# Edge sums in batches of four tiles, and a node ranking moved to another stage

## The reference

```python
# graph convolution of layer 0
agg[dst] = sum over edges (x @ W)[src] / sqrt(deg)
# attention layers (layers 1 and 2 have two each, layer 3 one)
w    = exp(e - m[dst])                       # one factor per edge and head
z    = segment_sum(w, dst)
out  = segment_sum(w[:, :, None] * xW[src], dst) / z[dst]
```

```python
perm = jnp.argsort(deg + deg_noise, stable=True)
```

## Time and profile before

| | |
|---|---|
| time, median of 3 runs | 10034.75 us (10032.0 to 10036.96) |
| span of the profiled execution | 10033.8 us |
| mean granted TensorE clock, share of 2.4 GHz | 0.734 |
| TensorE busy | 7411.3 us, 74% |
| VectorE busy | 5241.3 us, 52% |
| ScalarE busy | 2745.4 us, 27% |
| GpSimd busy | 3592.3 us, 36% |

### The profile page before, as it was taken

How to read it: one execution, slowest core, us unless ns; L and a number is a source line. 1 busy time by engine, 2 the same in 40 slices (tenths; PEclk the granted TensorE clock), 3 DMA queues, 4 the chain that set the end, 5 groups by cost and what they waited for, 6 DMA issues and landing times. The chain is left out here.

```text
span 10033.8 us, 106861 instructions
## 1 busy us (share of the span) xinstructions
PE 7411.3 (74%) x29302; PEld 4772.6 (48%) x29302; DVE 5241.3 (52%) x12836; ACT 2745.4 (27%) x6151; POOL 3592.3 (36%) x3597
## 2 busy tenths in 40 slices
PE   6867686996686596799679849848467469947756
PEld 6833333444454465477456536624223256623334
DVE  7832674225887556301475655555399575543221
ACT  0122000223674232122244314312232144412211
POOL 3715573002573574200536537600100236600111
PEclk5578656998898575799865557568689765568878
DMA  4200332002563432154233233300000133300012
GB/s 109 66 6 13 103 105 63 29 29 78 155 203 113 124 104 59 42 173 159 79 99 92 73 113 110 89 2 15 28 0 0 41 113 93 92 22 4 8 64 80
DMA packets 439924, 740.35 MB, mean 74 GB/s; under 512 B 172477, under 2 KB 268700, under 8 KB 437426
## 3 DMA queue, kind: packets, MB, share of 16 engines
q0 software_dynamic: 182080, 437.26, 15.8%
q1 hardware_dynamic: 239123, 276.05, 8.7%
q10 hardware_dynamic: 18136, 20.19, 0.6%
HBM read 659.96 MB, written 72.93 MB: 73 GB/s over the span
## 5 line engine op out<-in xcount | busy, mean ns | idle before, releaser
L2490 DVE TENSOR_TENSOR acc<-acc,PS 125x256 f32 (+4 forms) x2080 | 883.3, 425 | 1122.4 <-PE PS L2512 1043.3
L2448 POOL DMA_INDIRECT R<-table,edges x1248 | 1210.4, 970 | 611.3 <-issue 317.2
L2511 PEld LDWEIGHTS PS<-TW,hot 128*125 128x125 f32 x3328 | 852.3, 293 | 678.3 <-DVE hot L2470 549.6
L2448 POOL DMA_INDIRECT room<-table,edges x832 | 797.0, 958 | 588.1 <-PE PS L2512 552.3
L2512 PE MATMUL PS<-room,hot 128*125 128x256 f32 x1664 | 995.1, 701 | 0.0
L2512 PE MATMUL PS<-R,hot 128*125 128x256 f32 x1664 | 843.2, 612 | 106.1 <-DVE hot L2470 43.9
L2511 PE MATMUL PS<-TW,hot 128*125 128x1 f32 (+3 forms) x3328 | 762.7, 300 | 46.7 <-DVE hot L2470 15.6
L2464 ACT ACTIVATE R<-R,TW 128x128 f32<-128x128 f32 (+1 forms) x1664 | 611.0, 419 | 414.8 <-DMA R<-table,edges 408.8
L2470 DVE TENSOR_TENSOR hot<-iota,edges 128x125 f32<-128x125 f32 x2496 | 705.9, 284 | 31.3 <-PEq L71 30.5
L2268 PE MATMUL PS<-S,hotT 125*128 125x100 bf16 (+1 forms) x6240 | 352.7, 215 | 450.3 <-DVE hotT L2375 439.7
L2464 ACT ACTIVATE room<-room,TW 128x64 f32<-128x64 f32 x1664 | 479.1, 339 | 657.6 <-DMA room<-table,edges 654.9
(11 more groups left out here) (703 smaller groups left out, 12923.5 us busy)
## 6 DMA issues: line engine op xcount, KB each, us to landing
rowb<-slo_row SPq DMA_DIRECT2D x260, 250.0 KB
W<-in_L_ffn_W1p SPq DMA_DIRECT2D x32, 1024.0 KB
W<-in_L_ffn_W2p SPq DMA_DIRECT2D x32, 1024.0 KB
near<-dst_row SPq DMA_DIRECT2D x98, 256.0 KB
R<-table,edges POOLq DMA_INDIRECT x1248, 2.8
W<-in_L_ffn_w SPq DMA_DIRECT2D x16, 1024.0 KB
room<-table,edges POOLq DMA_INDIRECT x832, 2.8
hib<-hi_mask SPq DMA_DIRECT2D x260, 50.0 KB, 5.9
```

The source lines that it names most:

```text
L2448: pool.indirect_dma_start(self.R[:, u, 0:self.W], None, self.table[:, :], bass.IndirectOffsetOnAxis(ap=self.G.edges[:, g, 0:1], axis=0)).t ...
L2490: v.tensor_tensor(to, to, self.G.PS[0:P, k, 0:self.WH], ALU.add).then_inc(self.put, 1)
L2511: pe.matmul(self.G.PS[0:P, k, self.W:self.WH], self.hot[g % HOT][:, :], self.TW[:, g, :], start=True, stop=True)
```

## The change

- One-hot matrices of four tiles (`TB`) are made by one instruction of 500 elements, two batches ahead, in three buffers.
- VectorE scales its heads of four tiles in one instruction (512 elements in S3 and S5). In S1 it now has two heads of four, 1,024 elements, and ScalarE two. The instruction waits for all four tiles to have landed.
- The factors are copied into `R` behind the rows in all attention passes, by VectorE, and TensorE has one product per tile instead of two in the narrow ones. S1 has three pairs of banks instead of two.
- VectorE's order is now: one-hots of batch `b + 2`, factors and scaling of `b + 1`, the four adds of `b`.
- In the narrow passes and S0 TensorE makes a product of constants (bf16, 500 columns, into PSUM bank 7, which nobody reads) after every tile, and 16 of them at the start.
- The ranking moves from S0 to `bn_ffn`: its key row is stored and loaded after expert 1's weights have been issued, and each of 25 steps is halved (`below`, `above`) and put behind the add of a chunk, from chunk 2 to chunk 51.

```diff
-HOT, TB = 12, 4
+HB, TB = 3, 4
@@ bn_ffn, SyncE and TensorE
                             sp.dma_start(W[j][l][:, :, :], ...).then_inc(loaded[j], 16)
+                        if e == 1:
+                            ranking.sync(sp)
...
+                ranking.tensor(pe)
@@ bn_ffn, VectorE
+                ranking.start(v)
...
                             v.wait_ge(out_done, n + 1)
+                            if 2 <= n < 2 + 2 * T:
+                                (ranking.above if n % 2 else ranking.below)(v, (n - 2) // 2)
                         v.sem_inc(exp_done, 1)
+                ranking.finish(v)
+                v.tensor_copy(G.place[:, :], place[:, :])
@@ EdgeSums
-        self.banks = 2 if self.wide else 5
+        self.banks = 3 if self.wide else 5
-        self.split = 0 if H == 1 else 1 if self.wide else H // 2
+        self.split = 0 if H <= 1 else H // 2
+    def one_hots(self, v, b):
+        if b >= HB:
+            v.wait_ge(self.summed, (b - HB + 1) * TB)
+        v.tensor_tensor(self.hot[b % HB][:, :, :], self.G.iota[:, :].unsqueeze(1).to_broadcast([128, TB, P]),
+                        self.G.edges[:, b * TB:(b + 1) * TB, 2:3].bitcast(F32).to_broadcast([128, TB, P]),
+                        ALU.is_equal).then_inc(self.hot_done, 1)
+    def scale(self, v, b):
+        if not self.H:
+            return
+        g, n = b * TB, self.split
+        u = g % self.slots
+        if g >= self.slots:
+            v.wait_ge(self.summed, g + TB - self.slots)
+        v.tensor_copy(self.R[:, u:u + TB, self.W:self.WH], self.TW[:, g:g + TB, :]).then_inc(self.tails, 1)
+        if n:
+            for j in range(TB):
+                self.landed(v, g + j)
+            r = self.R[:, u:u + TB, 0:n * self.C].rearrange("p t (h c) -> p t h c", h=n)
+            v.tensor_tensor(r, r, self.TW[:, g:g + TB, 0:n].unsqueeze(3).to_broadcast([128, TB, n, self.C]), ALU.mult).then_inc(self.low, 1)
@@ EdgeSums.tensor
-            if self.H:
-                pe.matmul(self.G.PS[0:P, k, self.W:self.WH], self.hot[g % HOT][:, :], self.TW[:, g, :], start=True, stop=True)
-            mm = pe.matmul(self.G.PS[0:P, k, 0:self.W], self.hot[g % HOT][:, :], self.R[:, u, :], start=True, stop=True)
+            mm = pe.matmul(self.G.PS[0:P, k, 0:self.WH], hot, self.R[:, u, :], start=True, stop=True)
         mm.then_inc(self.summed, 1)
+        if not self.wide:
+            keep_clock(pe, self.G)
+def keep_clock(pe, G):
+    pe.matmul(G.PS[:, 7, 0:4 * P], G.ident_b[:, :], G.iota_b[:, :].unsqueeze(1).to_broadcast([128, 4, P]), start=True, stop=True)
@@ aggregate, VectorE and TensorE
-                for g in range(3):
-                    sums.one_hot(v, g)
-                for g in range(ET):
-                    if g + 3 < ET:
-                        sums.one_hot(v, g + 3)
-                    sums.scale(v, g)
-                    if g:
-                        sums.add(v, g - 1)
-                    if ranking and g % 15 == 14 and g >= 30 and (g - 30) // 15 < T:
-                        ranking.step(v, (g - 30) // 15)
+                sums.one_hots(v, 0)
+                sums.one_hots(v, 1)
+                sums.scale(v, 0)
+                for b in range(NB):
+                    if b + 2 < NB:
+                        sums.one_hots(v, b + 2)
+                    if b + 1 < NB:
+                        sums.scale(v, b + 1)
+                    for g in range(b * TB, (b + 1) * TB):
+                        sums.add(v, g)
...
+                for _ in range(0 if sums.wide else 16):
+                    keep_clock(pe, G)
```

More of the change, by code:

```diff
@@ L1069, in bn_ffn @@
         V = lambda x: G.small("L0_ffn_" + x)
+        place = s.sb("place", [P, T])
+        ranking = Ranking(G, s, G.key, place)
         with nc.Block() as block:
@@ L1196, in step, with below @@
     def step(self, v, t):
+        self.below(v, t)
+        self.above(v, t)
+    def below(self, v, t):
         if t == 0:
@@ L1205, in step, with above @@
             c(v.tensor_scalar(junk[:, 0:a], row[:, 0:a], k, 0.0, ALU.is_le, ALU.add, accum_out=part[:, 0, t:t + 1]))
+        c(v.tensor_scalar(junk[:, a:b], row[:, a:b], k, 0.0, ALU.is_lt, ALU.add, accum_out=part[:, 2, t:t + 1]))
+    def above(self, v, t):
+        c, row, junk, part = self.c, self.row, self.junk, self.part
+        k = self.key[:, t:t + 1]
+        a, b = t * P, (t + 1) * P
         if t < T - 1:
             c(v.tensor_scalar(junk[:, b:N], row[:, b:N], k, 0.0, ALU.is_lt, ALU.add, accum_out=part[:, 1, t:t + 1]))
-        c(v.tensor_scalar(junk[:, a:b], row[:, a:b], k, 0.0, ALU.is_lt, ALU.add, accum_out=part[:, 2, t:t + 1]))
         c(v.scalar_tensor_tensor(out=junk[:, a:b], in0=row[:, a:b], scalar=k, in1=self.G.after[0:P, 0:P],
@@ L2430, in __init__ @@
         self.wide = self.WH > 512
-        self.banks = 2 if self.wide else 5
+        self.banks = 3 if self.wide else 5
         self.C = W // H if H else W
-        self.split = 0 if H == 1 else 1 if self.wide else H // 2
-        width = self.WH if self.wide else W
+        self.split = 0 if H <= 1 else H // 2
         if room is None:
-            self.R = s.sb("R", [128, slots, width])
+            self.R = s.sb("R", [128, slots, self.WH])
         else:
-            self.R = room[:, 0:slots * width].rearrange("p (u w) -> p u w", u=slots)
-        self.hot = [s.sb(f"hot{j}", [128, P]) for j in range(HOT)]
+            self.R = room[:, 0:slots * self.WH].rearrange("p (u w) -> p u w", u=slots)
+        self.hot = [s.sb(f"hot{j}", [128, TB, P]) for j in range(HB)]
         self.got = [s.sem(f"got{j}") for j in range(slots)]
@@ L2456, in scalar @@
             return
-        u, W, C = g % self.slots, self.W, self.C
-        if self.wide and g % TB == 0:
-            if g >= self.slots:
-                act.wait_ge(self.summed, g + TB - self.slots)
-            act.activation(self.R[:, u:u + TB, W:self.WH], self.TW[:, g:g + TB, :], ACT.Copy).then_inc(self.tails, 1)
+        u, C = g % self.slots, self.C
         self.landed(act, g)
@@ L2492, in tensor @@
     def tensor(self, pe, g):
-        u, k, half = g % self.slots, g % self.banks, self.WH // 2
-        pe.wait_ge(self.hot_done, g + 1)
+        u, k, half, b = g % self.slots, g % self.banks, self.WH // 2, g // TB
+        hot = self.hot[b % HB][:, g % TB, :]
+        pe.wait_ge(self.hot_done, b + 1)
         if self.H:
-            if self.wide:
-                pe.wait_ge(self.tails, g // TB + 1)
+            pe.wait_ge(self.tails, b + 1)
             pe.wait_ge(self.high, g + 1)
         if self.split:
-            pe.wait_ge(self.low, g + 1)
+            pe.wait_ge(self.low, b + 1)
         if not self.H:
@@ L2506, in tensor, with aggregate @@
             for a in range(2):
[L2507 to L2512 removed]
+                mm = pe.matmul(self.G.PS[0:P, 2 * k + a, 0:half], hot, self.R[:, u, a * half:(a + 1) * half], start=True, stop=True)
+        else:
+            mm = pe.matmul(self.G.PS[0:P, k, 0:self.WH], hot, self.R[:, u, :], start=True, stop=True)
         mm.then_inc(self.summed, 1)
[L2516 removed]
+        if not self.wide:
+            keep_clock(pe, self.G)
+def keep_clock(pe, G):
+    pe.matmul(G.PS[:, 7, 0:4 * P], G.ident_b[:, :], G.iota_b[:, :].unsqueeze(1).to_broadcast([128, 4, P]), start=True, stop=True)
+def aggregate(nc, G, sums, early=0, own=None):
+    NB = ET // TB
     with Stage(nc) as s:
@@ L2721, in _ @@
             def _(v):
-                v.tensor_tensor(key[:, :], G.out_deg[:, :], G.noise[:, :], ALU.add).then_inc(steps, 1)
+                v.tensor_tensor(G.key[:, :], G.out_deg[:, :], G.noise[:, :], ALU.add).then_inc(steps, 1)
                 v.tensor_scalar(dg[:, 0, :], G.out_deg[:, :], 1.0, None, ALU.max).then_inc(steps, 1)
```

29 lines of the change are left out of this document (3 added, 26 removed).

## The result

The changed kernel takes 9929.4 us (median; 9928.09 to 9936.44), the kernel before 10,035.3: ratio 0.9896, 95% interval 0.9882 to 0.991. That is 106 us less, where 46 were forecast.

A forecast was written before the change was run, and what follows sets the result against it. GpSimd's gathers, at least 1.25 us a tile, were taken to set the pace, except in S3 and S5, held by TensorE. Terms: -164 passes, +16 ranking, +102 held gathers = -46, so 9,988 (median 9,989); range 9,885 to 10,085.

The forecast's parts named there:

- their new length: S3 and S5: gathers come down to 1.258 us a tile; -75 and -71 us with 10 each for held gathers.
- the high clock held: TensorE, all six passes: products of constants keep the granted clock near 1.00, so a tile stays under 1.25 us.
- their ends: S3 and S5: last add 16 us after the last gather began, instead of 34.5 and 39.8; -18.5 and -24 us.
- the rule for held gathers: Gathers behind long VectorE operations last longer by operation's end less own start less 0.12 us; +102 over the passes.
- VectorE's batch in S1: S1: a VectorE batch takes 5.2 us, 1.30 a tile, level with 1.29 before; VectorE becomes co-bound.
- The seven borders: Gated network: seven of 50 ranking halves lie on the path at expert borders, where ScalarE waits for `cur`; +16 us.
- rival 1: All passes: long VectorE operations miss the gathers nearly everywhere; -148 + 20, about 9,906 us; chance 0.23.
- S1 42: S1: gathers held by long VectorE operations, hit or miss by chance, add 42 us, VectorE's own 1.30 hiding a part.
- +6: S1 without held gathers: 6 us longer with its end, as VectorE's batch becomes co-bound.
- a mean gather above 1.05 us in S1: Sign for S1: gathers' mean above 1.05 us; a mean of 0.95 would make the forecast wrong.
- The start products: Sixteen products at a pass's start take 6.7 us at the low clock; S2 to S5 start 5.3 us later each, S0 nothing.
- its sum for a tile at the low clock: TensorE, narrow passes: 1.27 - 0.33 + 0.42 + about 0.1 = 1.46 us a tile, over 1.25, so the clock decides.

The follow-up runs named there:

- padded run: The changed kernel with eight more copies of 128x16 per batch on VectorE in S1, into tiles nobody reads: 9998.6 us, S1 613.8 us.
- the split alone: The changed kernel with one head of S1 on VectorE and three on ScalarE, instead of two and two: 9939.5 us, S1 551.4 us.
- split and one-input one-hots together: The changed kernel with one S1 head on VectorE, one-hots with one SBUF input, `cur` copied ahead, no start products: 9869.7 us, 0.9837; S1 544.5 us.

## Why the prediction was off

**Right.** What bounded S3 and S5, their new length (sums of -75 and -71, measured -79.9 and -75.7), the high clock held (0.88 to 0.98, if not "near 1.00" everywhere), their ends (16 us after the last gather; 15.0 and 14.8), and the rule for held gathers in the narrow passes (+18 in S4, +15.8 measured). VectorE's batch in S1 was worked out at 5.2 us and measured 5.11. The seven borders: ScalarE's waits for `cur` grew from 40.6 to 56.3 us in all, 15.7 where 16 was worked out.

The time lay inside the range and between the forecast and rival 1 (9,906). But rival 1's mechanism, gathers that are missed nearly everywhere, isn't what happened: they were held, in S1 as well, where 103 of 104 one-hots and 102 of 104 scalings ran across a gather's start. The one-hots did the holding (101 gathers, 0.15 us each on the mean); of the long scalings, on which the forecast's 42 us mostly rested, all but 7 ended too soon after the gather's start to lengthen it by over 0.06 us. So the size of the gain is a failed term and not the doing of rival 1.

**The step that failed.** "I take ... S1 42 (VectorE's own 1.30 hides a part)". It added held gathers to a pass whose pace VectorE already set. A held gather costs there only what makes GpSimd later than VectorE, and that was nothing; had the step taken the larger of the two instead of their sum, S1 would have had +6 and the whole -88. Of the 11 us then left, the six passes lie 24 below their sums, the gated network and everything else 13 above. The sign named for it, a mean gather above 1.05 us in S1, didn't come either: it was 0.988. The warning stood in the earlier trace rows: the median gather of S1 was 975 ns already before, against 946 in S0 and S2, so about half of them were held, in a kernel whose one-hots and scalings last 0.28 us; the mean was 986 ns then, and 988 after. The two beats were close there too (by the four one-hots 5.20 us at the median), and the long operations changed only who did the holding. The padded run shows it from the one side; the split alone, and split and one-input one-hots together, from the other.

**Smaller misses.** Held gathers in S2 cost 13 us (981 less the undisturbed 946 ns, x 367) where 18 were taken. The start products delayed S2 to S5 by 2.7 to 4.3 us, not 5.3. The ranking cost 22.9 and not 16: in four of seven cases TensorE, idle for 2.3 to 4.7 us at the border, came back at the lower clock (the window from 1881.7 on, above), and the chunk there took 1.5 to 2.3 us more; in the other three, idle for 1.9 to 3.2 us, it didn't. The 6.1 us of everything else, the sum of six stretches that changed by -2.8 to +3.1 us, stay unexplained.

**The clock didn't decide.** The forecast said so because its sum for a tile at the low clock, 1.46 us, holds 0.42 for the product that is there to keep the clock high. Without it the same sum gives 0.94 to 1.04 us, under 1.25: the merged factors needed no products on a quiet chip (S3 and S5 at 0.72 and 0.74 of the clock took 521 and 514 us). That S3 and S5 came out as forecast doesn't show that the high clock was needed.

## What to carry to other kernels

Where two engines have nearly the same beat, work out both paces and take the longer; a delay that one causes the other is then not a term of its own, and taking away only one of the two shows the other. When a change has several parts that lift the same ceiling, price each alone: here the products of constants alone gave 168 us, the whole change on the same chip 100. Batching saves VectorE time only where VectorE is short of it; elsewhere its long operations with two SBUF inputs lengthened GpSimd's gathers, and operations with one input did not.

## What the hardware showed that was not expected

- A VectorE operation with two SBUF inputs lengthened a gather that began inside it by what was left of the operation less 0.12 us (446 of 463 in the changed kernel, to within 0.03 us). Adds with one of their inputs in PSUM, and one-hots of the same 0.28 us with one input, lengthened none.
- Without a gap of over 0.31 us between two, GpSimd's gathers took on VectorE's beat: four of them took 5.17 and 5.76 us on the mean of S1, where VectorE's undisturbed batch was 5.11 and 5.73.
- TensorE, at 1.00 before the border and idle for 4.15 us there, was granted 0.50 for the next 4.8 us and 1.00 again later. Idle stretches of 2.8 and 3.2 us at two other borders left it at 1.00, one of 2.3 us didn't.
- The same kernel took 10,033 us on some chips and 11,068 and 11,131 on others, with 62 unexplained stops of TensorE in S3 of the changed kernel instead of one, and which of two versions is better depended on it.
